# Transposes through 512-byte-aligned buffers, and new instruction orders, in a four-layer cross-attention kernel

## The reference

```python
# layers 0 and 2 ("g")                              # layers 1 and 3 ("m")
xn = rmsnorm(x, norm_w)                             q = hidden_states @ Wq
q = (xn @ wq); k = cond @ wk; v = cond @ wv         k = ctx @ Wk; v = ctx @ Wv
scores = einsum('btgrd,bsgd->bgrts', qg, k)*scale   logits = einsum('bhqd,bhkd->bhqk', q, k)*scale + col_bias
attn = softmax(scores)                              probs = softmax(logits)
out = einsum('bgrts,bsgd->btgrd', attn, v)          out = einsum('bhqk,bhkd->bhqd', probs, v)
return residual + out @ wo                          return out @ Wo + bo + residual
x = L0(x, ctx); x = L1(x, ctx); x = L2(x, ctx); x = L3(x, ctx)
```

## Time and profile before

| | |
|---|---|
| median of 3 executions | 1936.2 us (1930.68 to 1937.98) |
| the profiled execution | 1937.18 us, its span 1934.6 us |
| busy shares of the span | PE 94%, DVE 84%, POOL 78%, ACT 74% |
| granted TensorE clock | 0.973 of full speed on average |
| DMA packets | 1168206, 320.31 MB, 166 GB/s on average |

### The profile page before, as it was taken

One profiled execution on the slowest core, in us unless ns is written; L12 is line 12 of the kernel. 1 busy time (PEld: TensorE's weight loads), 2 busy tenths in 40 slices (PEclk: granted clock), 3 DMA queues, 4 the chain that ended last, 5 costly groups with the idle time before them and its releaser, 6 DMA issues.

```text
span 1934.6 us, 72375 instructions
## 1 busy us (share of the span) xinstructions
PE 1813.3 (94%) x28144; PEld 1567.9 (81%) x28272; DVE 1622.0 (84%) x3322; ACT 1422.5 (74%) x2539; POOL 1508.7 (78%) x1880
## 2 busy tenths in 40 slices
PE   5699999999999999999999999999999999999995
PEld 5578888888888888888888888888888888888874
DVE  7688988898888998888888988888888898888873
ACT  3477777777877777777777777777877777777762
POOL 3478887788878888888888888788887888888863
PEclk7699999999999999999999999999999999999997
DMA  5289999999999999999999999999999999999995
GB/s 163 53 144 168 172 174 168 174 159 174 170 174 171 179 173 175 175 170 172 174 174 178 170 170 172 171 166 174 166 173 174 171 170 169 164 172 171 164 167 109
DMA packets 1168206, 320.31 MB, mean 166 GB/s; under 512 B 1140246, under 2 KB 1164124, under 8 KB 1167868
## 3 DMA queue, kind: packets, MB, share of 16 engines
q1 hardware_dynamic: 1167868, 315.69, 99.4%
HBM read 15.93 MB, written 4.19 MB: 10 GB/s over the span
## 4 chain that ended last, share of the span: by engine, by line
PE 68%; SPq 12%; DMA 6%; POOL 4%; issue 4%; DVE 2%; ACT 2%; ACTq 0%; POOLq 0%
PE ring L1205 36%; PE sc L1342 8%; SPq L485 6%; PE o_ps L1205 6%; DMA arena<-arena 5%; PE ring L1414 4%; PE o_ps L1360 4%; PE sc L1325 3%; SPq L517 2%; SPq L471 2%; PE sc L1340 1%; PE ring L1400 1%; SPq L504 1%; POOL p_sm L640 1%; PE ring L1276 1%
## 5 line engine op out<-in xcount | busy, mean ns | idle before, releaser
L635 POOL TENSOR_TENSOR p_sg<-arena,p_sg 128x512 f16<-128x512 f32 (+1 forms) x256 | 347.7, 1358 | 195.4 <-ACT p_sg L702 195.3
L1205 PE MATMUL ring<-ctx_four,m_w 128*128 128x154 f16 x6144 | 463.8, 230 | 0.8 <-DVE v_tile L898 0.6
L1205 PEld LDWEIGHTS ring<-ctx_four,m_w 128*128 128x128 f16 x6144 | 427.2, 96 | 1.5 <-DVE v_tile L898 0.8
L1080 DVE TENSOR_TENSOR arena<-sc,row_max 128x616 f32<-128x616 f32 (+2 forms) x512 | 407.0, 795 | 8.9
L640 POOL TENSOR_TENSOR p_sm<-arena,p_sm 128x616 f16<-128x616 f32 x256 | 337.8, 1320 | 40.5 <-ACT p_sm L702 40.4
L702 ACT ACTIVATE arena<-ring 128x462 f16<-128x462 f32 (+1 forms) x384 | 196.5, 512 | 182.0 <-PE ring L1205 181.9
L663 POOL TENSOR_TENSOR arena<-arena 128x1024 f16<-128x1024 f32 x128 | 273.9, 2140 | 17.7 <-ACT arena L702 17.7
L1205 PE MATMUL ring<-wv_m,ctx_four 128*103 128x512 f16 (+1 forms) x1152 | 280.1, 379 | 0.2
L1342 PE MATMUL sc<-arena,x_s 128*128 128x512 f16 (+1 forms) x1152 | 262.2, 336 | 6.8
L1059 DVE TENSOR_TENSOR arena<-ring,arena 128x462 f16<-128x462 f32 (+1 forms) x384 | 222.5, 579 | 14.3 <-ACT arena L702 9.0
L1077 DVE TENSOR_REDUCE row_max<-sc 128x6 f32<-128x462 f32 (+2 forms) x384 | 225.0, 586 | 6.0 <-PE sc L1342 4.9
(11 more groups left out here) (165 smaller groups left out, 3702.3 us busy)
## 6 DMA issues: line engine op xcount, KB each, us to landing
v_fourth<-v_tile SPq DMA_DIRECT2D x64, 105.6 KB
ctx_nat<-in_ctx_dram SPq DMA_DIRECT2D x64, 77.0 KB
x_nat<-in_x_dram SPq DMA_DIRECT2D x64, 64.0 KB, 2.6
arena<-p_sg SPq DMA_TRANSPOSE x256, 4.0
arena<-p_sm SPq DMA_TRANSPOSE x256, 4.8
out_dram<-y_out SPq DMA_DIRECT2D x64, 64.0 KB, 2.3
v_fourth<-v_tile SPq DMA_DIRECT2D x32, 101.6 KB
arena<-in_L_xattn_Wk_dram SPq DMA_DIRECT2D x2, 1024.0 KB, 5.9
```

Of the source, the lines that this page charges most:

```text
L635: pool.tensor_tensor(p_sg[k][:, LO, 0:e - a], probs_flat[:, a:e], p_sg[k][:, HI, 0:e - a], ALU.subtract).then_inc(sems["pg_lo"], 1)
L1080: dve.tensor_tensor(shifted[:, hs, :], s_view[:, hs, :], row_max[:, hs].unsqueeze(2).to_broadcast([P, hs.stop - hs.start, S]), ALU.subtrac ...
L1205: ins = pe.matmul(out, a, b, start=(n == 0), stop=(n == len(passes) - 1))
```

## The change

Two things are changed. First the placement: a filler `to_512` of 96 float32 (384 bytes) is put first, then `p_sm`, `p_sg0`, `p_sg1` and `arena`, and within `arena` the pieces `p_tm`, `p_tg`, `o_s`, `o_t` come first, each a multiple of 512 bytes long. From the sizes declared ahead of them, and with the filler as what lacked to a multiple of 512, the transposes' sources and destinations now all start at multiples of 512 bytes in a partition. Before, by the same sums, `p_sm` and `p_sg` started 416 bytes past one, `p_tm`, `p_tg`, `o_s` and `o_t` 320 bytes past one. Every operand started at a multiple of 32 bytes before too.

Second the orders of all five streams, with `ring_uses` following. No instruction is added or removed in the steady part.

```diff
+        sb("to_512", [P, 96], F32)
+        p_sm = sb("p_sm", [P, 2, 2, HALF, P], F16)
+        p_sg = [sb(f"p_sg{k}", [P, 2, (b1 - b0) * P], F16) for k, (b0, b1) in enumerate(G_BLOCKS)]
+        arena = sb("arena", [P, ARENA], F32)
         wq_r = [sb(f"wq_r{n}", [P, 2, R, KVG, 4, GD], F16) for n in range(2)]
...
         taken[0] = 0
+        p_tm = in_arena(2 * H * T, F16).rearrange("p (k a h t) -> p k a h t", k=2, a=2, t=T)
+        p_tg = [in_arena(2 * (b1 - b0) * T, F16).rearrange("p (a b t) -> p a b t", a=2, t=T) for b0, b1 in G_BLOCKS]
+        o_s = in_arena(2 * NOC * P, F16).rearrange("p (a n) -> p a n", a=2)
+        o_t = in_arena(2 * NOC * T, F16).rearrange("p (a c t) -> p a c t", a=2, t=T)
+        o_n = in_arena(NOC * P, F32)
         g_s = [in_arena(4 * HS, F16).rearrange("p (a t h s) -> p a t h s", a=2, t=2, s=S) for n in range(2)]
...
-ARENA = 15180
+ARENA = 15232
```

The new order of TensorE's `pair`, as the diff has it:

```diff
+                if exists(it, m - 4):
+                    values_m(it, m - 4)
+                if exists(it, g - 2):
+                    pick_values(it, n, g - 2)
+                if exists(it, g):
+                    scores_g(it, g)
                 if exists(it, g - 4) or exists(it, m - 4):
                     rest_and_turn(it, n, g - 4)
-                if exists(it, m - 6):
-                    output_m(it, n, m - 6)
-                if exists(it, g):
-                    scores_g(it, g)
                 if exists(it, lead):
                     folded(it, n, lead, chunks[0])
                     folded(it, n, lead, chunks[1])
+                if exists(it, m - 6):
+                    output_m(it, n, m - 6)
...
+                if exists(it, g - 4):
+                    output_g(it, n, g - 4)
                 if exists(it, m):
                     scores_m(it, m, 0)
+                    scores_m(it, m, 1)
                 if exists(it, g + 2):
                     keys_values(it, n, g + 2)
-                if exists(it, m):
-                    scores_m(it, m, 1)
+                    queries(it, n, g + 2)
                 for j, k in value_chunks(n)[0:1]:
                     if exists(it, j):
                         context_values(it, n, j, k)
-                if exists(it, g):
-                    pick_values(it, n, g)
-                if exists(it, g + 2):
-                    queries(it, n, g + 2)
                 if exists(it, m):
                     scores_m(it, m, 2)
-                if exists(it, m - 2):
-                    values_m(it, m - 2)
-                if exists(it, g - 4):
-                    output_g(it, n, g - 4)
```

More of the change, by code:

```diff
@@ L213, in ring_uses @@
         lead, chunks = fold_work(n)
-        return [("ot", g - 4, 0), ("ym", m - 6, 0), ("g", lead, chunks[0]), ("g", lead, chunks[1]), *[("ct", g + 4, 0)] * (layer(g + 4) == 0 or n % PAIRS == CT_EXTRA),
-                ("g", lead, chunks[2]), ("kv", g + 2, 0), *[("v", j, k) for j, k in value_chunks(n)[0:1]], ("vp", g, 0), ("q", g + 2, 0),
-                ("yg", g - 4, 0), *[("v", j, k) for j, k in value_chunks(n)[1:2]]]
+        return [("vp", g - 2, 0), ("ot", g - 4, 0), ("g", lead, chunks[0]), ("g", lead, chunks[1]), ("ym", m - 6, 0),
+                *[("ct", g + 4, 0)] * (layer(g + 4) == 0 or n % PAIRS == CT_EXTRA), ("g", lead, chunks[2]), ("yg", g - 4, 0), ("kv", g + 2, 0), ("q", g + 2, 0),
+                *[("v", j, k) for j, k in value_chunks(n)[0:1]], *[("v", j, k) for j, k in value_chunks(n)[1:2]]]
     RING = 3
@@ L275, in build @@
         bo = sb("bo", [P, 2], F32)
-        arena = sb("arena", [P, ARENA], F32)
         taken = [0]
@@ L310, in build @@
         probs_flat, shifted_flat = [t.rearrange("p h s -> p (h s)") for t in (probs, shifted)]
[L311 to L315, removed]
         ident = sb("ident", [P, P], F32)
@@ L359, in build @@
         v_mha = v_tile + [v_fourth]
-        p_sm = sb("p_sm", [P, 2, 2, HALF, P], F16)
-        p_sg = [sb(f"p_sg{k}", [P, 2, (b1 - b0) * P], F16) for k, (b0, b1) in enumerate(G_BLOCKS)]
         ms = sb("ms", [P, 2], F32)
@@ L534, in pair @@
                 g, m = 2 * n, 2 * n + 1
-                if exists(it, m - 2):
-                    turn_m(it, m - 2, 1)
+                if exists(it, g - 2):
+                    turn_g(it, g - 2, 1)
                 if exists(it, m - 2) and part(m - 2) != 3:
                     move_values(it, m - 2)
+                if exists(it, m - 2):
+                    turn_m(it, m - 2, 0)
+                    turn_m(it, m - 2, 1)
                 if exists(it, m - 4):
@@ L542, in pair @@
                     turn_g(it, g, 0)
-                    turn_g(it, g, 1)
-                if exists(it, m):
-                    turn_m(it, m, 0)
                 if layer(g + 4) == 0 and exists(it, g + 4) and exists(it + 1, g + 4):
@@ L672, in pair @@
                     low_part(it, g, 0)
+                    low_part(it, g, 1)
                 if layer(g + 4) == 0 and part(g + 4) == 3 and exists(it, g + 4):
                     context_parts(it, g + 4)
+                if exists(it, m + 2):
+                    x_parts(it, m + 2)
                 if exists(it, g + 2):
                     spread_keys(it, g + 2)
-                if exists(it, g):
-                    low_part(it, g, 1)
                 if exists(it, g + 4):
                     x_parts(it, g + 4)
+                if exists(it, m):
+                    low_part(it, m, 0)
                 if exists(it, g):
                     pack_values(it, g)
[L683 to L686, removed]
                 if exists(it, m):
@@ L848, in pair @@
                     folded(it, n, lead, chunks[0])
+                if exists(it, m - 4):
+                    high_out(it, m - 4)
+                if exists(it, lead):
                     folded(it, n, lead, chunks[1])
+                if layer(m - 6) == LAYERS - 1 and exists(it, m - 6):
+                    last_layer(it, n, m - 6)
+                if exists(it, g):
+                    exponential_g(it, g, 0)
                 if layer(g + 4) == 0 and exists(it, g + 4):
@@ L852, in pair @@
                 if exists(it, g):
-                    exponential_g(it, g, 0)
                     high_g(it, g, 0)
@@ L856, in pair @@
                     folded(it, n, lead, chunks[2])
-                if exists(it, g + 2):
-                    keys_values(it, n, g + 2)
                 if exists(it, g):
@@ L861, in pair @@
                     high_g(it, g, 1)
+                if exists(it, g + 2):
+                    keys_values(it, n, g + 2)
+                    queries(it, n, g + 2)
                 for j, k in value_chunks(n)[0:1]:
@@ L864, in pair @@
                         values(it, n, j, k)
-                if exists(it, g + 2):
-                    queries(it, n, g + 2)
-                if exists(it, g):
-                    picked_values(it, n, g)
                 if exists(it, m):
                     exponential_m(it, m, 0)
-                    high_m(it, m, 0)
                 for j, k in value_chunks(n)[1:2]:
@@ L875, in pair @@
                 if exists(it, m):
+                    high_m(it, m, 0)
                     exponential_m(it, m, 1)
+                if exists(it, g):
+                    picked_values(it, n + 1, g)
+                if exists(it, m):
                     high_m(it, m, 1)
-                if layer(m - 4) == LAYERS - 1 and exists(it, m - 4):
-                    last_layer(it, n + 1, m - 4)
                 if exists(it, g - 2):
                     turned(it, n + 1, g - 2)
-                if exists(it, m - 2):
-                    high_out(it, m - 2)
             for n in range(-3, PAIRS):
@@ L1148, in pair @@
                     maximum_g(it, g)
+                if exists(it, lead):
+                    folded(it, n, lead, chunks[0])
+                if exists(it, g):
                     shift_g(it, g, 0)
@@ L1152, in pair @@
                 if exists(it, lead):
-                    folded(it, n, lead, chunks[0])
+                    folded(it, n, lead, chunks[1])
                 if layer(g + 4) == 0 and exists(it, g + 4):
                     first_x(it, n, g + 4)
-                if exists(it, lead):
-                    folded(it, n, lead, chunks[1])
                 if exists(it, g):
                     shift_g(it, g, 1)
+                if exists(it, g - 2):
+                    normalise_g(it, g - 2)
+                if exists(it, g - 4):
+                    finish_g(it, n, g - 4)
                 if layer(g + 4) == 0 and exists(it, g + 4):
                     turn_context(it, n, g + 4)
-                if exists(it, g - 2):
-                    normalise_g(it, g - 2)
+                if exists(it, lead):
+                    folded(it, n, lead, chunks[2])
                 if exists(it, m):
                     maximum_m(it, m, 0)
-                if exists(it, lead):
-                    folded(it, n, lead, chunks[2])
+                    maximum_m(it, m, 1)
+                    shift_m(it, m, 0)
                 if exists(it, g + 2):
```

(11 more changed lines are left out.)

## The result

The changed kernel takes 1863.01 us (median of 4, 1862.7 to 1863.98) against 1937.09 us (1930.68 to 1939.83) for the one before in the same comparison: a ratio of 0.962, 95% interval 0.960 to 0.965.

What follows compares the result with a forecast made beforehand. TensorE was taken as near its floor, idle mainly where output_m waits for turn_out behind a nearly full SP. Removing 49.8 us in rounds and about 4 at the end, leaving 8: 1937.2 - 54 + 8 = 1891, so 1890 us; range 1868 to 1922.

Steps and rivals of the forecast that it cites:

- What bounds the kernel: Whole kernel: TensorE busy 1813.3 of 1934.6 us; its idle time in the rounds is output_m waiting for turn_out, SP nearly full.
- Only its idle 0.44 us a pair can be won: Rounds: TensorE works 13.71 of 14.15 us a pair, near its floor, so only the idle 0.44 us is removable.
- the 49.8 us: Seven rounds: TensorE's idle time, 1584.8 - 1535.0 us, all counted as removable.
- Left over: 8: Rounds: waiting expected to remain after the change, 6 us for the score banks and 2 us for ring waits.
- Start and end: Outside the rounds: latency, taken as they are, +-5 us; about 4 us of the end up to 1860 us removable.
- Aligned transposes ... without a term of its own: Transposes: gain from none to landing 5.4 to 4.3 us, issue 2.93 to 1.58; acts through the same idle 0.44 us.
- much faster (under 1872): Rival, chance 0.08: start and end shrink by more than 10 us, or TensorE's pieces come nearer to their columns.
- The sign of being wrong: Rounds whose TensorE busy time itself changes, which would mean transposes and matmuls touch each other; no size given.
- The windows: Profile windows: 1584.8 us taken as seven rounds, 226.4 us a round, 14.15 us a pair, TensorE working 13.71.
- VectorE and the score banks: At scores_g: the new order leaves 0.2 us to spare for shift_m emptying sc; 6 us set aside.
- output_m later: TensorE's output product: deadline moves by 3.1 us, slack won 2.44 to 3.1, covering all but one or two of 47 waits.
- The rule on descriptors: Transposes' reads off 256-byte boundaries: 8 beats become 13 (p_sm) or 10 (o_s); by it the queue empties about a third.

## Why the prediction failed

**What bounds the kernel.** Right: the waiting was at one place, for `turn_out`, behind an SP stream with little to spare. The experiments that shorten the transposes without touching an order remove it.

**"Only its idle 0.44 us a pair can be won": wrong, and this is the step that failed.** The prediction took all that TensorE's rows call busy for work that no wait touches. Part of it went together with the waits. In the seven rounds 57.7 us went, where the sum had 49.8 - 8 = 41.8. By their causes:

*The start of each wait, about 7.7 us.* A wait's end is visible in the rows, its beginning is not: in the earlier trace rows the small transpose starts at 1057.61 and is shown 0.31 us long, and 2.00 us of idle time follow it up to 1059.91. Without a wait the next product starts after 0.14 us, as the chain of waits of the kernel after shows:

```profile
1013.06 0.18 PE ring L1205 x6
1013.25 0.14 PE ring L1395
1013.39 0.68 PE ring L1205 x10
```

So the wait was 2.30 - 0.14 = 2.16 us and 0.16 of it were counted as busy. Over the 48 waits of the seven rounds (43.6 us by the view, none after) that is 7.7 us.

*The clock, about 6.8 us.* This is an estimate: four stretches of 3.4 us at half the clock held 1.7 us of work each, so that each cost 1.7 us. The changed kernel has none in its rounds. That the waits brought the clock down isn't shown by an experiment, but with the order of before the runs with the sources aligned have no such stretch in the rounds, and the one with only the destinations aligned has two.

*A hole in the trace, -6.0 us.* Not all of the 49.8 us was idle time. Half of the records of one product are missing from the trace of before, and the holes stand as idle time in front of L1342:

```profile
L1342 PE MATMUL sc<-arena,x_s 128*128 128x512 f16 x672 | 181.2, 378 | 6.0
...
L1340 PE MATMUL sc<-bias_r,bias_l 128*128 128x512 bf16 x112 | 42.1, 376 | 0.0
```

In the rounds of the kernel after, the second of these has all its records:

```profile
L1340 PE MATMUL sc<-bias_r,bias_l 128*128 128x512 bf16 x224 | 84.9, 379 | 0.0
```

*"Left over: 8": wrong.* It was 6 us for the score banks and 2 for the ring, and the view lists no wait of TensorE in the rounds. With the orders alone it lists none at the score banks either, but for 0.4 us of "issue".

Summed up for the rounds: 41.8 forecast - 6.0 (holes) + 8 (left over) + 7.7 (starts of waits) + 6.8 (clock) = 58.3, against 57.7 measured.

That the fall in TensorE's busy time is no effect of the order is settled by the run with the placement alone. Its 112 pairs, cut at the same instruction, take 1539.3 us, and TensorE's busy time in them is 1529.5 instead of 1545.3 us, with the same records missing. Nor did the products themselves get shorter with the aligned transfers: the most frequent one, 154 columns wide, has a mean of 230 ns before and 229 after. What the order does to single products is small and goes both ways. The float32 product of `output_g` took 315 ns before and with the placement alone, and takes 295 in the new order:

```profile
L1400 PE MATMUL ring<-o_tg,wo_g 128*128 128x128 f32 x222 | 51.8, 315 | 0.0
```

```profile
L1400 PE MATMUL ring<-o_tg,wo_g 128*128 128x128 f32 x222 | 47.4, 295 | 0.0
```

That is 222 x 20 ns = 4.4 us less, but another float32 product, L1317 in `scores_g`, rose from 240 to 250 ns, 2.2 us more. Which property of the neighbours matters wasn't tested.

**Start and end: mis-sized.** 15.4 us against 4, the other large miss. About 3.6 of them lie before the first cut. In the end, the chains of waits are shorter and the time at the lower clock is too: granted 0.96 on average in the last 202 us against 0.93 in the last 210 before. The parts weren't told apart. Together 45.8 forecast + 15.9 in the rounds + 11.4 outside = 73.1.

**"Aligned transposes ... without a term of its own": wrong.** I had argued that both halves act through the same idle time and so need not be told apart. By themselves they give 69.4 us (placement) and 40.6 us (orders), together 73. That they don't add is as argued; that the placement is the larger one was missed, since I bounded it by issue and landing times and then took the middle for nothing. The bounds that stood there (issue 2.93 to 1.58 us, landing 5.4 to 4.3 us, measured 2.00 and 4.5) hold what was needed against waits of a mean of 1.0 us: 0.9 us from the landing, and about 1 us more because SP gets to the transfer sooner. The orders alone take 1895.6 us, near the 1890 that I forecast for the whole, but that is in part luck: their waits are 21 us and not 8.

**The rival "much faster (under 1872)", given 0.08, came true.** It asked for start and end to shrink by more than 10 us, and they did. Its other condition, TensorE's pieces nearer to their columns, was met only where the clock no longer fell. The sign of being wrong that I had named, rounds with a changed busy time, did show, but it did not mean that transposes and matmuls touch each other.

**The windows.** The 1584.8 us that I took for seven rounds hold 1584.8 / 14.24 = 111.3 pairs, so a pair took 14.24 and not 14.15 us, and TensorE's rows 13.80 and not 13.71. Nothing in the sum hangs on it.

**VectorE and the score banks.** Right that it is no stall, though 6 us were set aside for one: VectorE waits for TensorE's scores, not the other way. Waits in the rounds of the kernel after; among TensorE's own there is no row at all.

```profile
DVE row_max L1079 <- PE sc L1342: 51.2, 229, 0.2
```

**output_m later.** Right in mechanism (its wait goes, all but 3.5 us, in the three runs that have the move), but it is cover that the aligned kernel hardly uses: with the placement alone 3.8 us are left there. In the new order it may be needed for the ring; the run with the product early doesn't answer that cleanly.

**The rule on descriptors.** The Trainium skill (DMA: Bandwidth & Descriptors, How a descriptor splits into AXI transactions) was the better guide than its constraint of 32 bytes for the DMA transpose (same page, Constraints): here the read side alone matters, and multiples of 256 bytes are enough. Beat counts worked out from it, an estimate, don't fit as well. They give 5 extra beats for `p_sm` and `p_sg` and 2 for `o_s`. But the fastest landing fell by 0.6 us for `p_sm` and 0.7 for `o_s` with as many runs. And the packets' time (share x span) is 1923 us before, 1874 with `o_s` aligned alone (99.0% of 1892.5) and 1689 with all sources aligned (90.6% of 1864.3). With 16 engines, 128 pairs and 2048 runs of `o_s` and 6656 of the others that is 49 x 16 / 262144 = 3.0 ns a run for the one and 185 x 16 / 851968 = 3.5 ns for the others, not 2 to 5. The figures are rough, for the packets' time also moves with the load: it is 1923 to 1929 us in the runs with no source aligned and 1653 to 1713 in those with all. A run that crosses a boundary seems to cost about the same wherever it crosses. Sources at other distances (64, 224 bytes for all) and plain copies of such runs would tell this apart; no run here shows either, so it stays open.

## What to carry to other kernels

Before covering the wait for a transfer by reordering, look whether the transfer can be made shorter: putting a DMA transpose's source on a multiple of the length of its runs (256 bytes here) cost one filler tensor and a new sequence of allocations and gave nineteen twentieths of the gain, and covering one reader in a full queue passed nearly half of the wait to the next. Don't take an engine's busy time for its floor where it waits often: here each wait hid its first 0.16 us in the modelled end of the instruction ahead, and four stretches at the lower clock, which a mean of 1.00 doesn't show, stood in it too. Before subtracting two windows, see that they hold the same work and the same records. And when two halves of a change act on the same idle time, price each alone before saying that the sum doesn't depend on which.

## What the runs showed that was not expected

The source's alignment changes not only when a transpose lands but how long SP is held by issuing it: 2.24 to 1.62 us in the median for 2048 runs, with the fastest issue nearly the same (1.52 and 1.48 us). The destination's alignment does nothing (2.24 us, 1935.6 us). And with sources aligned the same data moved at 178 GB/s in the rounds against 171, at a lower share of the engines' time (0.97 against 1.05).
